# Constant matmuls on TensorE around the border between two blocks of a two-layer transformer kernel

## What is computed

```
x = layernorm(x + L0_attn(x))    # 16 heads of 8, rms norm of q and k, softmax, projection
x = layernorm(x + L0_ffn(x))     # top-1 router, 16 experts 128 -> 512 -> 128 (gelu), capacity 320
x = layernorm(x + L1_attn(x))    # 16 heads, keys of 8, values of 64, causal, softmax, Wo 1024 -> 128
x = layernorm(x + L1_ffn(x))     # three cycles of a coupling net with gelu and sigmoid
```

## Time and profile before

| | |
|---|---|
| median of 3 runs | 844.42 us (841.54, 844.42, 844.48) |
| profiled execution, own time | 838.94 us |
| its span, first to last instruction | 837.2 us |
| mean granted TensorE clock | 0.961 of full speed |
| TensorE busy | 754.7 us, 90% of the span |
| VectorE, ScalarE, GpSimd busy | 520.6, 465.0, 311.9 us |
| `l0_layer` | 0 to about 235 us |
| `experts` | about 235 to 323.65 us |
| `second_layer` | 323.65 to 837.2 us |

### The profile page before, as it was taken

One profiled execution on the slowest core, in us unless ns is written; L12 is line 12 of the kernel. 1 busy time (PEld: TensorE's weight loads), 2 busy tenths in 40 slices (PEclk: granted clock), 3 DMA queues, 4 the chain that ended last, 5 costly groups with the idle time before them and its releaser, 6 DMA issues.

```text
span 837.2 us, 19481 instructions
## 1 busy us (share of the span) xinstructions
PE 754.7 (90%) x7228; PEld 421.4 (50%) x7228; DVE 520.6 (62%) x1401; ACT 465.0 (56%) x737; POOL 311.9 (37%) x466
## 2 busy tenths in 40 slices
PE   3799999998489993799999999999999999999992
PEld 2344444443257773245655555565555555566440
DVE  6488888886512112547656777666776665636556
ACT  3699998998322221256445555444554444554675
POOL 5124433443471003244433454334544323224505
PEclk9999999999779996599999999999999999999997
DMA  5344554433166542325234555235553224222003
GB/s 184 91 115 126 135 136 131 120 102 84 38 143 166 163 122 63 89 52 108 62 69 89 109 108 102 65 58 102 107 109 83 62 61 97 59 58 57 0 1 101
DMA packets 111737, 78.04 MB, mean 93 GB/s; under 512 B 12528, under 2 KB 103088, under 8 KB 111648
## 3 DMA queue, kind: packets, MB, share of 16 engines
q1 hardware_dynamic: 106256, 70.38, 34.7%
q0 software_dynamic: 3664, 5.70, 2.7%
q10 hardware_dynamic: 1728, 0.79, 0.4%
HBM read 37.86 MB, written 13.63 MB: 62 GB/s over the span
## 4 chain that ended last, share of the span: by engine, by line
PE 37%; SPq 10%; DVE 6%; DMA 3%; issue 3%; ACT 1%; POOL 1%; ACTq 0%; DVEq 0%; POOLq 0%
PE l_ps_c L1381 7%; PE l_ps_v L1408 7%; SPq L115 4%; SPq L113 4%; PE l_ps_v L1309 4%; PE l_ps_d L1394 4%; PE l_by_query L1330 2%; DMA q_ring<-l_max_rows 2%; PE l_by_query L1321 2%; DVE l_rden L1960 2%; PE l_by_key L1363 1%; PE l_by_key L1501 1%; PE l_ps_m L1298 1%; DVE l_neg_max L1948 1%; PE l_ps_m L1501 1%
## 5 line engine op out<-in xcount | busy, mean ns | idle before, releaser
L1948 DVE TENSOR_REDUCE l_neg_max<-l_by_query 128x6 bf16<-128x768 f32 x125 | 119.6, 957 | 123.9 <-PE l_by_query L1334 123.4
L2228 POOL TENSOR_SCALAR_AFFINE_SELECT l_probs<-l_probs 128x512 f32<-128x512 f32 x128 | 87.0, 680 | 201.9 <-ACT l_probs L1654 201.7
L535 ACT ACTIVATE l_probs<-l_ps_s,minus_bound 128x1024 f32<-128x1024 f32 x128 | 137.7, 1120 | 10.0 <-PE l_ps_s L392 8.8
L1654 ACT ACTIVATE l_probs<-l_by_key 128x768 f32<-128x768 f32 x128 | 103.7, 810 | 65.9 <-PE l_by_key L1366 61.7
L1381 PE MATMUL l_ps_c<-l_probs,l_values 128*64 128x256 f32 (+1 forms) x1024 | 112.3, 340 | 0.0
L1381 PEld LDWEIGHTS l_ps_c<-l_probs,l_values 128*64 128x64 f32 x1024 | 62.4, 136 | 39.0 <-issue 19.9
L407 PE MATMUL l_ps_o<-l_probs,l_vpad 128*32 128x256 f32 x1024 | 81.6, 391 | 0.3 <-ACT l_probs L535 0.3
L1675 ACT ACTIVATE l_values<-l_ps_v 128x512 f32<-128x512 f32 x64 | 38.2, 597 | 69.8 <-PE l_ps_v L1309 67.4
L1309 PE MATMUL l_ps_v<-w_v,l_xT 128*128 128x512 f32 x128 | 74.2, 662 | 0.4 <-ACT l_values L1675 0.4
L1408 PE MATMUL l_ps_v<-w_o,l_ctx 128*128 128x128 f32 x512 | 65.8, 282 | 0.0
L2236 POOL DMA_INDIRECT l_eg<-eout_d,fetch x32 | 34.9, 1092 | 76.4 <-POOLq L937 68.9
(11 more groups left out here) (288 smaller groups left out, 1392.6 us busy)
## 6 DMA issues: line engine op xcount, KB each, us to landing
l_rrep<-rden_d SPq DMA_DIRECT2D x32, 512.0 KB
q_ring<-l_parts SPq DMA_DIRECT2D x192, 64.0 KB
k_ring<-l_parts SPq DMA_DIRECT2D x180, 64.0 KB
w_both<-in_L_ffn_w_dram SPq DMA_DIRECT2D x32, 256.0 KB, 3.3
disp_d<-zeros SPq DMA_DIRECT2D x8, 320.0 KB, 4.1
l_xin<-in_L_attn_x_dram SPq DMA_DIRECT2D x16, 128.0 KB, 2.6
l_xr<-in_L_attn_x_dram SPq DMA_DIRECT2D x16, 128.0 KB, 2.5
x_d<-l_x SPq DMA_DIRECT2D x16, 128.0 KB, 2.8
```

What stands on the lines that cost most here:

```text
L535: act.activation(probs[c % RING][:, :], ps_s[c % 2][:, :], ACT.Exp, bias=k["minus_bound"][:, :], scale=SCALE).then_inc(probs_sb, 1)
L1654: act.activation(probs[c % P_RING][:, :, 0:N + P], by_key[:, :, 0:N + P], ACT.Exp, scale=SCALE).then_inc(p_sb, 1)
L1948: dve.tensor_reduce(neg_max[:, :, half, :, h].rearrange("p a u -> p u a"), query_scores(b, c)[:, :, 0:3 * P].rearrange("p u (a q) -> p u a ...
L2228: pool.affine_select(out=corners, in_=corners, compare_op=ALU.is_ge, fill=0.0, base=0, pattern=[[0, 4], [1, P]], channel_multiplier=-1).th ...
```

## The change

A helper `keep_awake` issues n matmuls, each with all 128x128 of `ident_bf` as weights and all 256 columns of `corner` as the moving side, into a PSUM bank that nobody reads at that time. It is called three times: 30 at the end of TensorE's work in `experts`, 60 at the head of `first_steps` in `second_layer`, and 10 after `queries_keys(1)`, ahead of the first `scores_by_query`, whose slots come by DMA. The loop over the two batches is written out, with the same order.

```diff
+def keep_awake(pe, k, bank, n):
+
+    for _ in range(n):
+        pe.matmul(bank[:, 0:2 * P], k["ident_bf"][:, :], k["corner"][:, :], start=True, stop=True)
@@ experts, TensorE
             pipelined(pe, step, 2, 0, E, W, first=2)
+            keep_awake(pe, k, ps_h[0][:, 0, :], 30)
@@ second_layer, TensorE
             def first_steps():
-                for b in two:
-                    x_by_channel(b)
-                    queries_keys(b)
+                keep_awake(pe, k, by_query[:, 0, :], 60)
+                x_by_channel(0)
+                queries_keys(0)
+                x_by_channel(1)
+                queries_keys(1)
+                keep_awake(pe, k, by_query[:, 0, :], 10)
                 for c in range(4):
                     scores_by_query(0, c)
                 values_of(0, 0)
```

## The result

The changed kernel takes 838.5 us in the median of 9 runs (836.64 to 842.51), the kernel before 842.42 us in the median of 9 (841.54 to 844.48): 3.9 us less, ratio 0.9947 with a 95% interval from 0.9926 to 0.9968. It is faster, by 0.53%, just beyond what the forecast called "within 0.5%". The forecast was 841.4 us and a gain of 3.0 us. (The ratio is estimated by itself and is not the quotient of the two medians. Taken by the ratio the gain is 4.5 us, with an interval from 2.7 to 6.2 us.)

The account below looks back on a forecast made before the run. TensorE was taken as the bound behind the second layer's head, so gains there arrive nearly whole. Terms 0 + 0 + 0 - 3.0 = -3.0 us, off the 844.42 us median of three runs, gave 841.4 us; range 838.0 to 846.0 us.

Parts of the forecast that it names:

- within 0.5%: Whole kernel: the outcome band of 4.2 us either way that a measurement can tell, given chance 0.64.
- The price of one constant matmul: Each added matmul on TensorE: 0.11 us at full clock, 0.22 us at half.
- The rival of loads that are not hidden: Constant matmuls: weight loads don't run beside the stream, 0.226 us each, about +5 us, 849.5 us; chance 0.07.
- The 30: Experts' end: 3.3 us of matmuls hidden behind the last store and the barrier; cost nothing.
- The 60: Second layer's head: 6.6 us of matmuls at full clock, done before the first transpose could start; cost taken as 0.
- Batch 0 and the 10: Ahead of the first scores: at most 0.7 us from batch 0 at full clock, eaten by the 10; net 0.
- What the 10 give: Scores and values: clock full from 342 to 343 us instead of 352.36 us, L1363 3.0 us sooner.
- Behind it: After the first scores by key: the clock falls again from 359.2 us, unaffected by the change; no term.
- a rival's term: Later fall at 359 us missed, saving 1.7 us, in the case that the clock never falls (-5.4 us); chance 0.13.

Follow-up runs that it names:

- e6: The change without the 30 constant matmuls at the experts' end (60 and 10 stay), against the kernel before: ratio 0.9902, on 4 runs.
- e11: Only the 30 constant matmuls at the experts' end, against the kernel before: ratio 0.9968, 2.7 us less.
- e7: The change plus 18 constant matmuls between the products of batch 0 and the transposes of batch 1, against the kernel before: ratio 0.9959.
- e2: The change without the 10 ahead of the first scores (30 and 60 stay), against the kernel before: ratio 0.9953, 3.9 us less.
- e9: The 30 and 60 without the 10, timed once more on another chip, against the kernel before: ratio 0.9945.
- e1: The changed kernel again, unaltered, on another chip, against the kernel before: ratio 0.9939, a gain of 5.1 us.
- e3: Only the 10 constant matmuls ahead of the first scores, against the kernel before: ratio 0.9964, 3.0 us less.
- e8: Only the 10, and 12 more in the wait for maxima ahead of maxima_by_head(0, 1), against the kernel before: ratio 0.9925, on 4 runs.
- e10: The change with 30 instead of 10 constant matmuls ahead of the first scores, against the kernel before: ratio 0.9971.
- e12: The 60, the 10 and 12 in the wait for maxima, without the 30, against the kernel before: ratio 0.9932, a gain of 5.7 us.

## Why the prediction was right or wrong

**The price of one constant matmul** was right: 60 in 6.72 us, 0.112 us each, with 60 loads beside them in 6.45 us. The rival of loads that are not hidden is out: one load and one matmul would have taken 0.226 us by its price. The rule of the Trainium skill that spoke for it (TensorE: Matmul & The Clock Gate, "What overlaps and what doesn't") does not hold for this shape: every one of these loads goes to all rows and is hidden all the same.

**The 30** ended at 324.99 us with the block starting at 325.72 us: hidden, as forecast. That they also gain nothing is only what the traces say (e6, e11); the timed runs of e11 gain 2.7 us.

**The 60** ended at 332.88 us, ahead of the transposes: cost nothing, as forecast. The clock stayed up over the gap between the 30 and the 60 in all traces that have both, and fell behind batch 0 in all of them but e7, as forecast.

**Batch 0 and the 10**: up to 0.7 us from batch 0, eaten by the 10, was right in kind, and "net 0" nearly. e2 and e9 show the first scores at 17.0 to 17.2 us without the 10, the change and e1 at 17.6 to 17.9 us, before at 18.1 us. The 10 overrun the slots by 0.4 to 0.9 us, and 0.2 to 0.5 us are left.

**What the 10 give**, the one term that counted, 3.0 us: its mechanism was right. The clock is back at the first scores and L1370 stands at 26.0 us against a forecast of 26.4 on this count (350.2 - 323.8), 3.3 us sooner than before. e3 shows that the 10 bring the clock back alone, e2 and e9 that the scores stay cold without them. The full 3.3 us are not the 10 alone: without the 60 it is 2.0 us in e3 (27.3 us) and 1.7 us in e8 (27.6 us), with ScalarE's slower issues in the chain. And in e1 and e6 the clock fell again ahead of L1370, which left 1.7 and 1.8 us. The size of 3.0 us so hit the one trace that it was compared with by some luck; over the traces with the 10 or more and the 60, the gain there runs from 0.9 us (e10) to 3.8 us (e7).

**Behind it**: the second cold stretch came again at the same step, as forecast, in this trace. The traces that have it lose 1.2 to 1.5 us there; a rival's term had 1.7 us. In e1, the same kernel, it did not come at this place.

**The steps that failed** are in the sum, and neither is the mechanism of the 10 in the trace. The measured median is 2.9 us under the forecast of 841.4 us. The first step is the level: a median of three, 844.42 us, was taken as the time from which 3.0 us go off. The median of nine is 842.42 us, so 2.0 of the 2.9 us are here. The scatter of 3 us within the three runs was in the table and went into the range but not into the middle. The forecast itself named the 5.5 us between that median and the profiled execution as a danger; the median of nine is 3.5 us above it.

The second step is the gain, 3.9 instead of 3.0 us, the other 0.9 us. The sum put the 30, the 60 and batch 0 at full clock at nothing, and so the effect came out as 0.36% of 844.42 us instead of 0.53% (0.61% in e1), and the chance of more than 0.5% as 0.28. What the runs put in place of that nothing: the 30 and 60 without the 10 gain 3.9 and 4.6 us in timed runs (e2, e9), the 30 alone 2.7 us (e11). With 3.0 us of the 10 alone (e3) that would be some 7 us together, and all together measured 4.5 and 5.1 us. Each of these gains has some 2 us to either side, so it is not shown that the parts don't add; and the interval of the result, 2.7 to 6.2 us, still holds the 3.0 us of the forecast.

Where the timed gain of e2, e9 and e11 comes from is only in part known. It is not the comparison, since before against itself gives 0.9992. Three things on record bear on it.

- The first trace of the kernel before was a short one, 3.5 us under the median of nine, and it is the one that the ends of the other traces were held against. If each trace's end is corrected by its distance from the median of its own timed runs (an estimate, which puts all of the distance into this block), the kernel before ends at 515.3 to 516.9 us, e2 at 513.2, e11 at 512.1 and e9 at 510.6 us: 2 to 4, 3 to 5 and 5 to 6 us less, which is near the timed gains of 3.9, 2.7 and 4.6 us. That is no finding about the place: where in the block it lies, no trace shows.
- In clock, the two traces of the kernel before are ordinary ones (0.961 and 0.963; the mean of 83 runs is 0.962). By this measure it does not draw bad places more often than they show. The trace of e11 is not ordinary: its timed runs are at half clock for 57.9 us on average, 5.6 us less than those of before on the same chip. At 0.36 to 0.46 us of time for each of them, an estimate from the scatter of the runs of before, that is 2.0 to 2.6 of its 2.7 us. For e2 this does not help: its timed runs have 51.7 us, its trace 51.9 us.
- About a quarter of a us of each gain lies outside the span. In e1 to e12, the time of a run exceeds its span by 1.7 to 1.8 us in all 108 runs of kernels with constant matmuls, and by 2.0 us on average (1.7 to 2.4) in the runs of the kernel before. Why is open.

One rival is untested: all the kernels with constant matmuls also have the loop over the two batches written out, and no run has only that. TensorE's other instructions and their order are the same, so nothing speaks for it but the quarter of a us, which all of them share.

## What to carry to other kernels

Ahead of a critical stretch that starts on TensorE behind a wait for DMAs, a few constant matmuls right before it, inside the wait, bring the clock back for that stretch, and many long ahead did not: here 10 of them (2 us) had it back some 7 to 15 us sooner. In time the two kinds can't be ranked (10 alone gain 3.0 us, 90 without them 3.9 and 4.6 us, each with 2 us to either side), but few were enough: 10 and 12 in a later wait gave a ratio of 0.9925, 112 gave 0.9926. Count them so that they end as the wait ends; 20 beyond it moved the first scores by 2.4 us. And where the runs of a kernel scatter by as much as the effect, put the middle of a forecast on the change and not on the level of three runs, and don't read the effect from the end of one profile but from a point close behind the change. Hold each profile's time against the median of its kernel first: the profile of before was 3.5 us under it here. And read the clock that each timed run lists, not only that of the profile.

## What was not expected of the hardware

The clock can fall where TensorE is mostly busy. In e1 it fell at 21.1 us (338.29 us in the trace), in a stage with 5.76 of 7.00 us busy and a clock of 0.74; in the 2.2 us before, TensorE had waited 0.56 and 0.30 us for maxima:

```profile
334.20:341.20 7.00, 5.76 (x42) 2.25 (x41) 4.49 (x7) 0.85 (x2) 1.15 (x1) 0.74 0.51 130
```

In e6, e7 and e9 it fell once within the steady loop, for 3.4 us each time, behind a wait of 1.8 to 1.9 us for a batch's rows. (e3 waited 2.2 us once and kept its clock.) So one late landing may be paid twice: once as a wait, and once as 3.4 us at half clock behind it; that the wait is the cause is argued from three traces, not shown. None of the kernels with the 12 in the gap had this, whose sums of such waits are 3.0 to 3.8 us; whether that is cause or chance is open.
